# Mamba stage: the next image loaded in 12 pieces between the spreads of C, and the first bf16 residue of B and C made by POOL instead of VectorE

## The reference, cut to what matters

```
xz = x @ W_in.T;  xi, z = xz[..., :d_inner], xz[..., d_inner:]
u  = silu(conv1d(xi) + conv_b)                     # d_inner = 128
x_dbl = u @ W_x.T
dt = softplus(x_dbl[..., :4] @ W_dt.T + b_dt)
B, C = x_dbl[..., 4:20], x_dbl[..., 20:36]         # 16 states each
h  = exp(dt * A) * h + (dt * u) * B                # a scan along the sequence, per state
y  = sum over states of h * C, + u * D_skip
out = y * silu(z) @ W_out.T
```

## Time and profile before

| | us |
|---|---|
| median of 3 runs | 6452.99 (6450.01 to 6456.59) |
| profiled execution | 6451.64 |
| its span | 6449.8 |
| VectorE busy, whole kernel | 5081.2 |
| POOL busy, whole kernel | 4686.1 |
| TensorE busy, whole kernel | 4509.5 |
| ScalarE busy, whole kernel | 2524.9 |
| first and last close (L1950) of the Mamba stage | 3351.6 and 6435.9 |

### The profile page before, as it was taken

How to read it: one execution, slowest core, us unless ns; L and a number is a source line. 1 busy time by engine, 2 the same in 40 slices (tenths; PEclk the granted TensorE clock), 3 DMA queues, 4 the chain that set the end, 5 groups by cost and what they waited for, 6 DMA issues and landing times. The chain is left out here.

```text
span 6449.8 us, 55394 instructions
## 1 busy us (share of the span) xinstructions
PE 4509.5 (70%) x15006; PEld 2441.9 (38%) x15006; DVE 5081.2 (79%) x4078; ACT 2524.9 (39%) x3885; POOL 4686.1 (73%) x3364
## 2 busy tenths in 40 slices
PE   4888656565564756553257888888788887887887
PEld 2666523332323333232123433433344343443433
DVE  4888726776766677666558989989899898998998
ACT  1112111111111111110056666666666666666664
POOL 1666617777777777777457878878788787887887
PEclk8777766566565665655589999999999999999999
DMA  5556723434435344343235444444444544444443
GB/s 156 116 120 128 146 73 104 123 115 143 122 104 153 104 122 121 119 124 105 87 113 150 151 144 149 152 144 150 143 155 142 153 151 146 149 138 154 154 152 117
DMA packets 377439, 853.16 MB, mean 132 GB/s; under 512 B 194828, under 2 KB 237732, under 8 KB 372784
## 3 DMA queue, kind: packets, MB, share of 16 engines
q1 hardware_dynamic: 292432, 618.03, 32.7%
q0 software_dynamic: 84672, 231.32, 11.9%
HBM read 766.91 MB, written 56.48 MB: 128 GB/s over the span
## 5 line engine op out<-in xcount | busy, mean ns | idle before, releaser
L2035 POOL TENSOR_TENSOR ma_hc<-ma_h,ma_cc 128x784 f32<-128x784 f32 x1024 | 1885.1, 1848 | 628.5 <-DVE ma_h L1937 496.4
L827 POOL DMA_INDIRECT fl_quad<-table,fl_idx x1764 | 1698.5, 963 | 694.4 <-issue 537.0
L1592 PE MATMUL ma_bank<-ma_hc,ident 128*128 128x392 f32 x4096 | 1529.9, 495 | 74.5 <-POOL ma_hc L2035 74.5
L1937 DVE TENSOR_TENSOR_SCAN ma_h<-ma_da,ma_state,ma_bank 128x784 f32<-128x784 f32 x768 | 1417.4, 1846 | 168.6 <-POOL ma_hc L2035 67.0
L1810 ACT ACTIVATE ma_da<-ma_dt,ma_a_neg 128x784 f32<-128x784 f32 x1024 | 948.1, 943 | 496.1 <-DVE ma_h L1937 479.3
L978 DVE TENSOR_TENSOR fl_part<-fl_quad,fl_bank 128x2304 f32<-128x2304 f32 x196 | 500.3, 2552 | 709.6 <-DMA fl_quad<-table,fl_idx 697.0
L1925 DVE TENSOR_TENSOR ma_bank<-ma_dtu,ma_bank 128x784 f32<-128x784 f32 x1024 | 980.7, 958 | 32.7 <-PE ma_bank L1579 32.2
L1592 PEld LDWEIGHTS ma_bank<-ma_hc,ident 128*128 128x128 f32 x4096 | 709.0, 190 | 504.1 <-POOL ma_hc L2035 79.0
L1119 PE MATMUL fl_bank<-ident,fl_tap 128*128 128x128 f32 (+1 forms) x980 | 242.8, 410 | 935.8 <-DVE xres L996 875.0
L1579 PE MATMUL ma_bank<-ma_bc,ma_sel 96*128 96x512 bf16 (+1 forms) x2048 | 517.0, 334 | 451.4 <-DVE ma_h L1937 439.9
L986 DVE TENSOR_REDUCE fl_tap<-fl_part 128x576 f32<-128x2304 f32 x196 | 796.6, 4064 | 0.1
(11 more groups left out here) (220 smaller groups left out, 6095.8 us busy)
## 6 DMA issues: line engine op xcount, KB each, us to landing
ma_cc<-c_rows SPq DMA_DIRECT2D x512, 784.0 KB, 4.2
mx_win<-flat SPq DMA_DIRECT2D x64, 878.0 KB, 10.2
fl_quad<-table,fl_idx POOLq DMA_INDIRECT x1764, 2.7
table<-fl_xt SPq DMA_DIRECT2D x64, 392.0 KB
mx_mask<-in_c_mask SPq DMA_DIRECT2D x56, 294.0 KB, 4.4
ma_xs<-ma_x SPq DMA_DIRECT2D x64, 196.8 KB, 5.2
ma_xs<-ma_x SPq DMA_DIRECT2D x64, 196.5 KB, 5.7
mx_xf<-flat SPq DMA_DIRECT2D x8, 816.0 KB, 15.5
```

The source lines that it names most:

```text
L827: gp.indirect_dma_start(quad[i][:, kk, :], None, table, bass.IndirectOffsetOnAxis(ap=idx[i][:, kk:kk + 1], axis=0))\
L1592: ins = pe.matmul(ps_y[:, t, :], ident[:], hc[:, n % RH, at], start=False, stop=(n == DS - 1))
L1937: dve.tensor_tensor_scan(h[:, i % RH, :], da[:, i % RH, :], ps_bu[i % 2], before, ALU.mult, ALU.add).then_inc(scand, 1)
L2035: gp.tensor_tensor(hc[:, i % RH, :], h[:, i % RH, :], cc[:, i % (NGRP * GRP), :], ALU.mult)\
```

## The change

Four edits, all in stage_mamba.

1. The image is loaded in 12 pieces. Pieces 0 to 7 are the eight DMAs of 8 shuffled rows, pieces 8 to 11 are 16 plain rows each. In chunk q = 1 they go between the spreads: 0 to 2 in the first group behind spreads 1 to 3 of the next group, 3 to 6 in the second group behind its spreads 4 to 7, 7 to 10 behind the next group's spreads 0 to 3, and 11 right behind piece 10. The wait for centred stands ahead of piece 0.
2. ScalarE's second copy takes all 96 rows to cs, and waits for the residue of the group before. POOL makes the residue from cs and bc, behind state 8. What POOL did behind states 8 to 11 moves one state later, and state 9 waits for the residue, state 12 for low_part. ScalarE's mid_part moves from slot 8 to slot 9.
3. Where PE waited for resid, because ps_f was still being read, it waits for high.
4. The waits ahead of times_b, scan and times_c are put in another order: in scan saved, hcd, expd, bud.

More of the change, by code:

```diff
@@ L1463, in period @@
                 Q = NQ * b + q
+                more = q == 1 and not (isinstance(b, int) and b == NB - 1)
+                if more:
+                    later = k["x3"][bass.ds(b + 1, 1)].rearrange("b c n -> (b c) n")
                 for g in range(2):
@@ L1481, in period @@
                             store(b, q - 1)
-            image(k["x3"][0])
+            for n in range(12):
+                piece(k["x3"][0], n)
             stack(0, 0)
@@ L1640, in period @@
                         if i == 10 and norm:
-                            pe.wait_ge(resid, START + F + 1)
+                            pe.wait_ge(high, START + F + 1)
                             if g == 0:
@@ L1921, in times_b @@
                 V = DS * G + i
-                dve.wait_ge(bready, START + V + 1)
                 if i == 0:
                     dve.wait_ge(dtud, START + G + 1)
+                dve.wait_ge(bready, START + V + 1)
                 dve.tensor_tensor(ps_bu[i % 2], dtu[g][:], ps_bu[i % 2], ALU.mult).then_inc(bud, 1)
@@ L1972, in period @@
                             close(G - 1, Q + g - 1, 1 - g)
-                        if i == 9 and ready:
-                            residue(F, 1 - g)
                         if i == 15 and g == 1 and post:
                             finish(Q - 1, (m - 1) % NQ)
-            residue(0, 0)
             chunks(dve, period)
@@ L2013, in low_part @@
                 if isinstance(F, int) and F == 0:
-                    gp.wait_ge(dtud, START + 1)
+                    gp.wait_ge(resid, START + 1)
                 else:
-                    gp.wait_ge(hcd, START + DS * (F - 1) + 11)
+                    gp.wait_ge(hcd, START + DS * (F - 1) + 12)
                 gp.wait_ge(midd, START + F + 1)
@@ L2023, in out_scale, with times_c @@
                 gp.tensor_tensor(xn[:], o[:], ors[:], ALU.mult).then_inc(xn_p, 1)
-            def times_c(G, i, after_low=None):
+            def times_c(G, i, after_low=None, after_left=None):
                 V = DS * G + i
                 j = i // GRP
-                gp.wait_ge(scand, START + V + 1)
                 if after_low is not None:
                     gp.wait_ge(lowd, START + after_low)
+                if after_left is not None:
+                    gp.wait_ge(resid, START + after_left)
                 if i % GRP == 0:
@@ L2034, in times_c @@
                     gp.wait_ge(yd, START + V - RH + 1)
+                gp.wait_ge(scand, START + V + 1)
                 gp.tensor_tensor(hc[:, i % RH, :], h[:, i % RH, :], cc[:, i % (NGRP * GRP), :], ALU.mult)\
@@ L2045, in period @@
                     for i in range(DS):
-                        times_c(G, i, after_low=(F + 1 if i == 11 and ready else 1 if i == 0 and older is False else None))
+                        times_c(G, i, after_low=(F + 1 if i == 12 and ready else 1 if i == 0 and older is False else None),
+                                after_left=(F + 1 if i == 9 and ready else None))
                         if i == 2 and g == 1 and post:
@@ L2051, in period @@
                         if i == 8 and ready:
+                            residue(F, 1 - g)
+                        if i == 9 and ready:
                             correct2(F)
-                        if i == 9 and ready:
+                        if i == 10 and ready:
                             step_size(F, 1 - g)
-                        if i == 10 and ready:
+                        if i == 11 and ready:
                             low_part(F, 1 - g)
-                        if i == 11 and ready:
+                        if i == 12 and ready:
                             step_product(F, 1 - g)
@@ L2067, in _ @@
             step_product(0, 0)
+            residue(0, 0)
             low_part(0, 0)
```

## The result

The changed kernel takes 6306.73 us (median of 4, 6304.29 to 6309.37) against 6452.05 of the kernel before: the ratio is 0.9774, 95% interval [0.9757, 0.9791]. Faster was forecast, 6268 us with 6250 to 6335 as the range; the time lies in it, but 39 us above the forecast. The profiled execution took 6309.37 us.

What follows compares the result with a forecast made beforehand. VectorE was taken to set the pace. From 6451.6 us, minus 91.9 (image), 44.7 (residue) and 56 (order of waits), plus 5 (chains) and 3.6 (start), came 6267.6, said as 6268 us; range 6250 to 6335.

Steps and rivals of the forecast that it cites:

- The pace: In the Mamba stage's groups VectorE sets the pace, busy 45.07 of 47.69 us, with POOL at 39.12.
- The image: At the seven image loads in the loop, 12 pieces between spreads of C remove the whole stall, 91.9 us.
- Rival B: At the image loads, half the stall stays because pieces delay spreads or the last come late: 6314 us, chance 0.12.
- The residue: Moving the residue off VectorE saves 0.71 us a group, 44.7 us over 63 groups.
- The order of the waits: Ahead of scans, register operations run during VectorE's product once its wait is last: 1.00 us a looped group, 56 us.
- Rival A: The new order of waits gives nothing, since register operations stay behind the product: 6324 us, chance 0.10.
- The chains: POOL's chain to dtu has 0.2 us of slack, PE's close may wait 0.1 to 0.3 every second group: 5 us.
- The start: At the stage's start L2018 waits for the first residue and two casts: 3.6 us lost, ends 0 and 5.
- Rivals D and E: D: residue on POOL at three times 1.85 us, 6489, chance 0.02; E: POOL operation holds VectorE up throughout, 6385, 0.02.

Runs made afterwards that it cites:

- bud-second variant: The changed kernel with scan's waits as saved, bud, hcd, expd (saved, hcd, bud, expd for i < 4 in the loop): 6283.66 us, ratio 0.9743.

## Why the prediction was right, and where it was off

The forecast had 184 us of gain in the profiled execution, it was 142.3. The closes divide it: 49 clean groups 49 x 1.16 = 56.8, images 91.9 - 10.5 = 81.4, the other 14 intervals 10.4, the start -5.6 (first close at 3351.6 and 3357.2), the end -0.8.

1. **The pace.** VectorE sets it, POOL follows: right. POOL took the residue without VectorE waiting once for dtu.
2. **The image**, 91.9 us, measured 81.4; alone 79, and 81 when put back. The mechanism was right. Mis-sized: one group in eight is longer in both kernels where the loop turns, 0.7 us before and 1.1 after; the pieces don't touch that, and 91.9 had it inside. The rest is the one stretch of lower clock. The last pieces came in time: ScalarE never waited for them in the loop. Rival B is out.
3. **The residue**, 0.71 us a group: 0.74 and 0.61 measured alone, 0.68 in the loop in company. Right.
4. **The order of the waits**, 56 us. This is the step that failed. The prediction read the 0.09 us between loop and last image as a register operation standing behind the product, and took it to be gone once bud is last. It is gone. But bud last makes it the first semaphore of the event, and the look at the second one now stands behind the product on every state, 0.045 us each, in the loop and in the last image. In place of 1.00 us a group it brought 0.40 in the loop and -0.37 in the last image: 18 us by the medians of the two orders, about 20 by the closes. That is 38 us too few, and the forecast was missed by 39. The agreement is partly luck: the image's term came out 10 us short, and the residue with its chains and its start 11 us better (47 where 44.7 - 5 - 3.6 = 36 was said), and the two cancel. Rival A, 6324 us, was nearer than the forecast, by another mechanism than its own: the register operations did leave. That bud second brings back the 1.04 us is shown by the variant, which gains 23 us; in the loop's state 2 it failed to put bud second.
5. **The chains**, 5 us: about 3. On PE the prediction was right. The close starts 0.10 us later in every second group (0.1 to 0.3 was said), 28 x 0.10 = 3 us, and at the forecast's own pace 0.22, as the bud-second variant shows. On POOL nothing was lost: the slack at dtu is 1.0 us, not 0.2, since the scans are slower than reckoned and the residue is 1.67 us instead of 1.85.
6. **The start**, 3.6 us: from the first normalization to the first scan it is 52.15 against 48.54, 3.6 us. On top of it the first image's 12 pieces delayed the first normalization by 1.5 us (18.7 us after the first of them was issued, against 17.3), which had been left out, and the stage itself began 0.8 us later.

Rivals D and E are out: 1.67 us of residue, and scans of 1836 to 1849 ns.

```profile
L2026 POOL TENSOR_TENSOR ma_left<-ma_cs,ma_bc x64: 1662/1668/1676, 3292.7 to 6224.9; 96x784 f32<-96x784 f32 x64
...
L1952 DVE TENSOR_TENSOR_SCAN ma_h<-ma_da,ma_state,ma_bank x768: 1836/1847/1849, 3395.1 to 6287.4; 128x784 f32<-128x784 f32 x192
```

## What to carry to other kernels

Where a stall stands at a transfer that is late, look at what stands ahead of it in its queue and move that between transfers that have slack: the same 12 pieces cost 81 us in a block, and left no wait behind them when spread out. Moving an operation off the engine that sets the pace is worth the spacing it takes there, not its duration (0.71 of 0.96 us), and costs nothing elsewhere only as long as the chain behind it has slack; size that slack before counting on it. Of several waits ahead of an instruction that runs a thousand times, the one that comes last in time should be the last looked at, and the code's order need not be the order of looking: read it off the sequencer's rows.

## What the runs showed of the hardware

- A wait event with two semaphores takes 50 ns behind the late one when that stands first in it, and one with the late one alone 21 ns: 1.09 us from product to scan with the late one first of two, 1.04 with it second, 23 us over 1024 scans and what followed them.
- Eight DMAs of 8 rows of 12.25 KB (784 KB), with 8 packets under way together over 13.6 us, behind which 7 to 9 us are lost; and one DMA of 64 such rows, the same bytes, with 16 together in 4 us, behind which nothing is.
- POOL's subtraction of bf16 from f32 over 784 columns takes 1.66 to 1.68 us, for 32 and for 96 rows. With both inputs in f32 and 128 rows five of its lines take 1.84 to 1.85 us and one, the product of x and rs (L1997 of the changed kernel), 1.57. So the runs do not show that the type is the cause.
